# Row maxima of attention computed on two halves of TensorE's rows

## The reference

```python
scores = jnp.einsum('bhqd,bhkd->bhqk', Q, K) / np.sqrt(D_HEAD)
causal = jnp.triu(jnp.full((t, t), -jnp.inf, dtype=scores.dtype), k=1)
attn = jax.nn.softmax(scores + causal, axis=-1)
O = jnp.einsum('bhqk,bhkd->bhqd', attn, V)
```

## Time and profile before

| what | us |
|---|---|
| median of 3 runs | 824.59 |
| the profiled execution | 822.99 |
| its span, first to last instruction | 821.3 |
| PE (TensorE) busy in the span | 714.6 (87%) |
| DVE (VectorE) busy | 673.1 (82%) |
| ACT (ScalarE) busy | 567.6 (69%) |
| POOL (GpSimd) busy | 408.0 (50%) |
| mean granted TensorE clock | 0.964 of 2.4 GHz |

### The profile page before, as it was taken

One profiled execution on the slowest core, in us unless ns is written; L12 is line 12 of the kernel. 1 busy time (PEld: TensorE's weight loads), 2 busy tenths in 40 slices (PEclk: granted clock), 3 DMA queues, 4 the chain that ended last, 5 costly groups with the idle time before them and its releaser, 6 DMA issues. The chain is left out here.

```text
span 821.3 us, 17279 instructions
## 1 busy us (share of the span) xinstructions
PE 714.6 (87%) x4289; PEld 322.1 (39%) x4345; DVE 673.1 (82%) x2283; ACT 567.6 (69%) x922; POOL 408.0 (50%) x496
## 2 busy tenths in 40 slices
PE   6768999999999999999999997887989889788656
PEld 4422333332333333333333332333556456455345
DVE  5979999898998988998989995336987989879793
ACT  4720377666766766776667666669998988988871
POOL 8881122231122213212311222556999999999972
PEclk9975799999999999999999999998999999999997
DMA  6984536344533643463355315001001101100000
GB/s 181 287 204 115 117 74 143 92 91 110 131 82 76 140 114 75 100 142 88 90 112 132 83 38 132 28 17 54 2 1 39 39 1 40 40 0 14 2 12 27
DMA packets 58955, 67.06 MB, mean 82 GB/s; under 512 B 15488, under 2 KB 33536, under 8 KB 58880
## 3 DMA queue, kind: packets, MB, share of 16 engines
q1 hardware_dynamic: 53120, 62.35, 32.0%
q10 hardware_dynamic: 5184, 2.36, 1.0%
q0 software_dynamic: 576, 1.57, 0.7%
HBM read 46.73 MB, written 19.53 MB: 81 GB/s over the span
## 5 line engine op out<-in xcount | busy, mean ns | idle before, releaser
L805 ACT ACTIVATE probs<-ps 128x384 f32<-128x384 f32 (+2 forms) x384 | 292.3, 809 | 179.0 <-PE ps L870 177.0
L770 POOL TENSOR_SCALAR_AFFINE_SELECT probs<-probs 128x256 f32<-128x256 f32 x256 | 103.0, 407 | 359.1 <-ACT probs L805 356.7
L956 DVE CUSTOM_DVE_ANT_0 junk<-ps,tri 128x256 bf16<-128x256 f32 (+3 forms) x512 | 228.6, 487 | 21.6 <-PE ps L838 18.4
L838 PE MATMUL ps<-QK 128*128 128x512 bf16 (+3 forms) x735 | 222.5, 343 | 26.3 <-DVE mx L960 12.4
L870 PE MATMUL ps<-Qa,Ka 128*128 128x512 bf16 (+3 forms) x745 | 175.0, 328 | 8.0 <-issue 2.5
L960 DVE TENSOR_REDUCE mx<-ps 128x1 f32<-128x512 f32 x256 | 162.0, 681 | 17.8 <-issue 10.1
L856 PE MATMUL ps<-probs,Vg 128*9 128x512 f32 (+3 forms) x1536 | 154.0, 490 | 0.0
L838 PEld LDWEIGHTS ps<-QK 128*128 128x128 bf16 x768 | 69.4, 97 | 214.1 <-DVE mx L956 87.8
L1123 POOL TENSOR_TENSOR QK<-front 128x1024 f32<-128x1024 f32 x60 | 115.8, 1951 | 0.0
L1231 ACT ACTIVATE ps<-QK,nb 128x512 f32<-128x512 f32 x128 | 83.2, 682 | 16.1 <-DVE A L1403 14.3
L1403 DVE SCALAR_TENSOR_TENSOR A<-QK,rows,ps 128x511 f32<-128x511 f32 x128 | 89.8, 738 | 3.0 <-ACT ps L1231 2.6
(11 more groups left out here) (138 smaller groups left out, 828.4 us busy)
## 6 DMA issues: line engine op xcount, KB each, us to landing
QK<-q_scr SPq DMA_DIRECT2D x48, 192.0 KB
QK<-k_scr SPq DMA_DIRECT2D x48, 192.0 KB
Qa<-q_scr SPq DMA_DIRECT2D x48, 192.0 KB
Ka<-k_scr SPq DMA_DIRECT2D x48, 192.0 KB
o_scr<-Os SPq DMA_DIRECT2D x32, 256.0 KB, 2.1
q_scr<-front SPq DMA_DIRECT2D x34, 128.0 KB, 3.5
k_scr<-front SPq DMA_DIRECT2D x18, 128.0 KB, 4.2
xin<-in_L_attn_x_dram ACTq DMA_DIRECT2D x8, 256.0 KB, 4.4
```

The costliest lines, as they stand in the source:

```text
L770: pool.affine_select(out=diag, in_=diag, compare_op=ALU.is_ge, fill=0.0, base=0, pattern=[[0, 2], [1, P]], channel_multiplier=-1).then_inc ...
L805: act.activation(probs[:, k % 2, hh, 0:width], ps[:, bank:bank + 2, :].rearrange("p a c -> p (a c)")[:, 0:width], ACT.Exp, scale=SM_SCALE) ...
L838: pe.matmul(ps[:, X_BANK + f % X_SLOTS, 0:c1 - c0], Qx[:, u, hh, P * i:P * (i + 1)], Kx[:, u, hh, c0:c1], start=True, stop=True).then_inc( ...
L956: dve.tensor_tensor_reduce(out=junk[:, f % 4, 0:w], in0=src, in1=tri[:, CHUNK - w:CHUNK], scale=1.0, scalar=-BIG, op0=ALU.add, op1=ALU.max ...
```

## The change

Two neighbouring heads of a group now use different halves of the array's rows for x: heads 0 and 2 rows 0 to 63, heads 1 and 3 rows 64 to 127. A half has room for 64 = 8 x 8 rows, so one of the nine products of parts (third part of q by third part of k) is left out for the maximum; the scores use nine as before. Each half is loaded by six DMAs of 16, 24 and 24 rows for two heads, twelve per group in place of six. The memsets of the padding rows go, and the waits on them. The built program gives each x a tile of 64 rows by 128 columns at row 0 or row 64, where before it had one of 128 by 128; s and p keep theirs (128 by 128, and 128 rows by 32 columns).

```diff
@@
-        Qx, Kx = [QK[:, GH * SEQ * w:GH * SEQ * (w + 1)].bitcast(BF16).rearrange("p (u h t) -> p u h t", u=2, h=GH)
+        Qx, Kx = [QK[:, HALF_HEADS * SEQ * w:HALF_HEADS * SEQ * (w + 1)].bitcast(BF16).rearrange(
+                      "p (u h t) -> p u h t", u=2, h=HALF_HEADS)
                   for w in range(2)]
@@
+        def load_halves(eng, u, g, done):
+            for a in range(2):
+                row = HALF * a
+                for r in range(PARTS):
+                    n = PARTS if r > 0 else PARTS - 1
+                    for dst, src in ((Qx, q_scr[g, a:GH:2, r:r + n]), (Kx, k_scr[g, a:GH:2, 0:n])):
+                        eng.dma_start(dst[row:row + DH * n, u, :, :],
+                                      src.rearrange("n h s d t -> (n s d) h t")).then_inc(done, 16)
+                    row += DH * n
@@
-                    sp.wait_ge(pads_made, 2)
-                    load_parts(sp, Qx[:, 0], Kx[:, 0], bass.ds(0, 1), xop_loaded[0])
+                    load_halves(sp, 0, bass.ds(0, 1), xop_loaded[0])
@@
-                    pool.memset(Kx[:], 0.0).then_inc(pads_made, 1)
@@
-                    dve.memset(Qx[:], 0.0).then_inc(pads_made, 1)
@@
                     def load_next_max(n, u):
                         sp.wait_ge(mx_read, CPG * (n - 1))
-                        load_parts(sp, Qx[:, u], Kx[:, u], bass.ds(n, 1), xop_loaded[u])
+                        load_halves(sp, u, bass.ds(n, 1), xop_loaded[u])
@@
-                        pe.matmul(ps[:, X_BANK + f % X_SLOTS, 0:c1 - c0], Qx[:, u, hh, P * i:P * (i + 1)],
-                                  Kx[:, u, hh, c0:c1], start=True, stop=True).then_inc(mx_ready, 1)
+                        rows = slice(HALF * (hh % 2), HALF * (hh % 2) + HALF)
+                        pe.matmul(ps[:, X_BANK + f % X_SLOTS, 0:c1 - c0], Qx[rows, u, hh // 2, P * i:P * (i + 1)],
+                                  Kx[rows, u, hh // 2, c0:c1], start=True, stop=True).then_inc(mx_ready, 1)
```

More of the change, by code:

```diff
@@ L27 @@
 M_ROW = SPLIT_ROWS
+HALF = P // 2
+HALF_HEADS = HEADS // HG // 2
 VW = DH + 1
@@ L87 @@
 LOADS = 6
+MAX_LOADS = 12
 ONE = 1
@@ L668, in m_rows @@
                             sp.dma_start(dst, src[blk]).then_inc(mrow_loaded[u], 16)
-                    load_parts(sp, Qx[:, 1], Kx[:, 1], bass.ds(1, 1), xop_loaded[1])
+                    load_halves(sp, 1, bass.ds(1, 1), xop_loaded[1])
                     store_parts(sp, BATCH - 1)
@@ L678, in _ @@
                             qk_stored[(2 * BATCH - 2 + u) % QS], 16)
-                    sp.wait_ge(pads_made, 5)
+                    sp.wait_ge(pads_made, 3)
                     load_parts(sp, Qa[:, 0], Ka[:, 0], bass.ds(0, 1), sop_loaded[0])
@@ L874, in _ @@
                     for f in range(CPG):
-                        max_chunk(0, f, 0, LOADS * 16)
+                        max_chunk(0, f, 0, MAX_LOADS * 16)
                     for f in range(AHEAD):
-                        max_chunk(CPG, f, 1, LOADS * 16)
+                        max_chunk(CPG, f, 1, MAX_LOADS * 16)
                     def early_sum():
@@ L924, in group @@
                                 elif f + AHEAD >= CPG and last < 1:
-                                    max_chunk(CPG * (n + 2), f + AHEAD - CPG, u, LOADS * 16 * (turn + 2))
+                                    max_chunk(CPG * (n + 2), f + AHEAD - CPG, u, MAX_LOADS * 16 * (turn + 2))
                                 f += 1
@@ L944, in _ @@
                     dve.wait_ge(v_staged, 3)
-                    dve.wait_ge(pads_made, 3)
+                    dve.wait_ge(pads_made, 1)
                     def max_chunk(base, f):
```

## The result

The changed kernel takes 847.75 us (median of 4 runs, 847.32 to 848.93) against 823.48 us for the kernel before in the same comparison: a ratio of 1.0296, with a 95% interval of 1.0262 to 1.033. That is 24 us slower.

A forecast was written before the change was run, and what follows sets the result against it. TensorE and VectorE each need 25.3 of 28.2 us a group, neither alone the bound. Tile changes +3.9, pairs -1.3, 1.1 hidden: 1.5 us over 14.3 groups, +21 on 823, so 844 us; range 812 to 864.

The forecast's parts named there:

- A change of tile costs 0.10 us: TensorE between x and s: each switch between 64-row and full tile loses 0.10 us, taken from p's tile.
- Rival A: Tile changes between x and s are free for a split of rows and pairs gain: 813 us, chance 0.25.
- 39 of them, 3.9 us a group, 1.1 us of the sum hidden: x and s adjoin 39 times a group: 3.9 us on TensorE; 1.1 of the 2.6 net of pairs hides in waits.
- Pairs give 1.3 us: Two x in a row on different row halves run side by side; half of 2.6 us a group comes back, 1.3.
- the net: TensorE in the interleaved groups: 3.9 less 1.3 is 2.6 us, of which 1.5 us lengthen each group.
- Twelve loads 0: SyncE issues twelve loads in 5.7 us instead of 2.84, covered by busy transfer queues: cost 0.
- memsets 0: The memsets at the kernel's start are covered by the first projections, so dropping them changes 0.
- start 0 to 1: The first x's wait for its load, till 53.94 us: 0 to 1 us either way, taken as 0.
- Rival B: Twelve issues on SyncE bring the maxima's rows late, up to 2.8 us a group: 851 us, chance 0.08.
- rival D: Half-height matmuls bring the 1.2 GHz clock into the loop: over 1,100 us, chance 0.04.

## Why the prediction was right

It said 844 us and slower; 847.75 was measured. Point by point:

- **A change of tile costs 0.10 us** (taken from p's tile, between bounds of 0 and 0.10). Shown: 99 and 106 ns behind the last column where it was 3 and 13, so 0.095 us net, and 72 rows on the old tile cost nothing. The prediction's sentence from the Trainium skill, "TensorEngine Tiling (Array Packing)", section Key Properties, on the drain at a change of mode is borne out for the 64-row tile: the next weights load only when the last column is through, while between the two halves (one shape) nothing is lost. Rival A (free change) falls, since the tile of x costs 28 us.
- **39 of them, 3.9 us a group, 1.1 us of the sum hidden.** 39 x 0.069 = 2.7 us exposed by the kernel with ten changes; the kernel without pairs gives 30.9 - 28.2 = 2.7 in the groups that the clock leaves alone. The prediction's 3.9 - 1.1 = 2.8 is near that. Its 1.1 was a guess from the waits and not worked out from a row, so that this term fits is in part luck. The wait list that the prediction read as the price (25.4 us in 89 waits at p) isn't one: 0.29 us a wait.
- **Pairs give 1.3 us.** The group grew by 29.91 - 28.14 = 1.77 us, 0.09 of it the clock's (1.2 us in thirteen groups, below); 2.7 exposed less 1.7 leaves 1.0. This term was a little too large, and makes the net 1.7 for the forecast's 1.5: 14.3 x 0.2 = 3 us. Half of the neighbours overlap (117 of 227), as the prediction took it, but what they free on TensorE isn't all a shorter group.
- **Twelve loads 0, memsets 0, start 0 to 1.** They gained 3.4 to 4.1 us (the two kernels with the old tile and twelve loads). Rival B falls: in the changed kernel no first s waits for Qa<-m_scr, and at the place shown the store comes back 1 us sooner behind the first load, though it is issued later.
- **The clock, rival D.** In the changed kernel it is small: 1.2 GHz lasts to 99.1 us in the first interleaved group, where it ended at 92.4 before, and comes back at 153.7 to 157.1. The first group is 3.3 us longer than in the kernel with the tile put back, some 1.5 more than the other groups are; the second stretch makes its group 1.2 us longer than others of its kind. That is about 3 us, which the prediction did not count. The first of the two is uncertain: in the six kernels with the full tile for x throughout, 1.2 GHz ended anywhere from 90.0 to 95.6 us. The reason for giving D little, that TensorE stays as dense in time, was wrong in itself: the kernel at row 0 throughout is recorded as busy for 336 of the 341 us from 114 on, with a mean clock of 0.61.

The sum: 25 for the groups (14.3 x 1.77, the clock's 1.2 among them), 1.5 for the clock in the first, less 3.4 for the loads and what goes with them: +23 of the 24. The cause and its price were forecast rightly. That 21 came within 4 us was luck in part: a gain that I had put at nothing (3.4) met a cost that I had put at nothing (the clock's 3).

## What to carry to other kernels

Count how often TensorE changes between tile shapes before splitting the array: each change from the 128-row tile to the 64-row one or to p's 32-column one, and back, cost 0.10 us here, some 240 columns, and 0.07 of it showed although VectorE was as much the bound. Short matmuls on a smaller tile, strewn among full ones, lost more than their pairs won (2.7 against 1.0 us a group). One shape for x and s took the price away, but brought the lower clock. Leaving rows empty (72 of 128 used) cost nothing. When a kernel moves to smaller tiles, read the granted clock before reading anything else.

## What the runs showed of the hardware that was not expected

**Half-height tiles and the clock.** Mean granted clock from 114 to 455 us: 1.00 in the kernel before and in the one with the tile put back; 0.99 in the changed kernel; 0.98 with x at row 0 alone and s full; 0.95 with x and s on 64-row tiles with pairs on both halves; 0.61 with both at row 0 and no pairs; 1.00 again when that kernel reads 128 rows. The less of the array's height the matmuls used, the more of the stretch ran at 1.2 GHz. What the engine did just before shows a second condition. All 14 falls to 1.2 GHz between 114 and 480 us, in six kernels with 64-row tiles, came during or within 4 us after an idle moment of TensorE of 0.55 to 1.7 us. In the changed kernel it stands at the head of an iteration, and the clock fell at 153.7:

```profile
152.11 0.28 PE L850 MATMUL ps<-QK 64*128 64x256 bf16 x1 [1.32 <-DVE mx L972]
```

In the six kernels with x and s on the full tile the same moments stand there, 1.00 us long in the earlier trace rows and up to 1.48, and the clock fell at none of them. So in these kernels a fall took the idle moment and the smaller tile together, and even then most of the moments passed without one (five of six in the changed kernel). Once down, the kernel at row 0 stayed at 1.2 GHz for 44 to 96 us at a time behind such a fall. The Trainium skill, "TensorE: Matmul & The Clock Gate", Part 1, says that the gate is set by how busy the engine was recently. The trace agrees as far as the falls go, which follow idle moments; it does not agree for the 49 us at 1.2 GHz of which TensorE was recorded as busy 48.7. Why the height matters no run here shows.

**Smaller loads were not slower.** Six loads of 24 rows and four heads, or twelve of 24 rows and two heads: the twelve took 5.6 us to issue instead of 2.8 and the kernel still gained 0.5% (ratio 0.9951, 0.9934 to 0.9967).
